# Writing a six-layer loop out, and moving one product and one normalisation in the drain of each layer

## The chip, the cores and the metric

The kernel runs on one core of a Trainium2 chip. The metric is device time in microseconds (us) of one execution. The core has five engines with an instruction stream each: TensorE (PE: matmuls, and PEld: its weight loads), VectorE (DVE), ScalarE (ACT), GpSimd (POOL) and SyncE (SP, which issues the DMAs). They meet through semaphores.

## The reference

Input x is 4 x 1024 tokens of width 128, all in float32. First comes one block of linear attention (16 heads, elu + 1 features) with a residual. Its layer-normalised result goes through a stack of six layers, and the stack's output is added to x:

```python
for i in range(6):
    x = attn_layer(shift_tokens(x), Wqkv[i], ...) + x      # 16 heads of 64, rotary, window of 32 plus the 32 before
    x = ffn_layer(shift_tokens(x), ln_g[i], ..., W2[i]) + x  # layer norm, 128 -> 2 x 341, a * gelu(gate), -> 128
```

In attn_layer q and k are l2-normalised, rotated, and the softmax runs over 64 keys for each query. shift_tokens delays half of the channels by one token.

## The kernel before

All x stays on the chip (x_tok). Work goes in tiles of 128 tokens: 32 tiles a layer (NT = 32), and for the feed-forward part in groups of four tiles (NG = 8).

**Front.** A software pipeline over the eight groups computes the linear attention. It holds small hardware loops of its own (schedule) and is not changed.

**Layers.** Every engine then runs its own hardware loop over the layers, `with engine.Fori(0, DEPTH) as l` (PE L476, DVE L920, ACT L1256, POOL L1519, SP L1663). The body is one layer, already written out tile by tile; only SP keeps inner loops. The layer number l is a register value, so semaphore targets such as NT * l + NT are computed in registers.

**Attention of a layer.** every_tile calls step(k) for k = 0 to 31 plus a drain of up to three more steps, and step(k) works on tile k in stage 0, tile k-1 in stage 1, and so on. Inside a step the order is written by hand on each engine; engines run in order and nothing reorders them. For tile 0 PE transposes the shifted tokens (L563), ACT and DVE split them into a high and a low part (xsT_hi, xsT_lo), PE projects q and k (L580 to L582), ACT squares them (L1324), DVE multiplies by the rotary tables (L1006, L1009) and makes the inverse norms, POOL adds and scales (L1542, L1551), PE transposes them (L594), computes scores (L632), and ACT takes exponentials (L1338), the first of them at k = 2. DVE and POOL normalise the probabilities (L993, L1531), PE transposes them (probs_transposed, L606), ACT copies them (p_evacuated), and PE multiplies by the values (output, L666). The values themselves come from products vo (L648), which ACT and DVE copy out of PSUM; a ring of four PSUM banks serves all these, so a product waits until its bank is copied.

**Drain and feed-forward.** Group 0 of the feed-forward part starts inside the drain. For group u: DVE centres it (L767, L769), ACT or DVE squares it, DVE takes the variance and a seed of the inverse root (L774 to L778), POOL runs twelve small Newton steps (group_rsqrt, L1454 to L1457), DVE writes the normalised tokens (normalised, L784), PE transposes them (L505), ACT and DVE split them, PE makes the up products up(u, par, i) for three blocks i of hidden columns (L525 to L527), ACT takes the gelu (L1396), DVE makes the hidden block (L1117), PE the down product (L539), and DVE the new x (L1125) with POOL's x plus bias xb (L1566).

In the drain PE runs up(0, 0, 0) at k = NT + 1, up(0, 0, 1) at k = NT + 2 ahead of the last tile's output, and up(0, 0, 2) after the residual of the last tile (x_mid). up(0, 0, 1) writes the two banks of the scores, so it waits for the last exponentials. DVE's normalised(0, 0) is called by every_tile ahead of step(NT + 1).

**Between layers.** The last products of a layer are wvo_product (L387), combined weights of the next layer; ACT copies them (wvo, L1161) and PE waits for all four copies before the next layer's first transpose.

**Activation tables.** ScalarE's functions sit in table sets. The build puts an ACT_TABLE_LOAD wherever the set that an instruction needs isn't known to be loaded there; at the head of a loop body nothing is known. Copy, Square and Identity run here under the set of Exp and under that of Gelu.

Of the kernel before, what the change touches and what calls it, by code (L numbers as in the profile page):

```python
# [35 lines left out]
NT = B * TPB  # L36
DEPTH, H, D, WIN = 6, 16, 64, 32
# [65 lines left out]
def build(nc, consts, at, x, Wq, bq, Wk, bk, Wv, bv, Wo, bo, Wqkv, q_scale, k_scale, Wout,  # L103
          ln_g, ln_b, W1, b1, W2, b2, out):
    ctx = ExitStack()
    with ctx:
# [217 lines left out]
        def every_tile(step, depth, before={}):  # L324

            for k in range(NT + depth):
                if k in before:
                    before[k]()
                step(k)
# [17 lines left out]
        def done(T):  # L347

            return passed(T + 1)
# [5 lines left out]
        def ahead(engine, value):  # L355

            engine.compute_val(value)
            return value
# [3 lines left out]
        def _(pe):  # L362
# [112 lines left out]

            with pe.Fori(0, DEPTH) as l:  # L476
                pe.wait_ge(x_ready, NT * l + NT)
# [67 lines left out]
                def step(k):  # L545
# [134 lines left out]
                    values(1, 1)  # L680
                    if k == NT + 2:
                        up(0, 0, 1)
                    output(3)
# [10 lines left out]
                    scores(0, 1)  # L694
                    probs_transposed(0, 2)
                    probs_transposed(1, 2)

# [36 lines left out]
        def _(dve):  # L734
# [184 lines left out]

            with dve.Fori(0, DEPTH) as l:  # L920
                dve.wait_ge(tables_ready, l + 1)
# [27 lines left out]
                def step(k):  # L949
# [149 lines left out]
                    rotate("k", 1, 0)  # L1099
                    softmax_bias(0, 1)  # L1100


# [40 lines left out]

                every_tile(step, 3, {NT + 1: lambda: normalised(0, 0)})

# [13 lines left out]
        def _(act):  # L1159
# [95 lines left out]

            with act.Fori(0, DEPTH) as l:  # L1256
                def step(k):
# [186 lines left out]
        def _(pool):  # L1444
# [46 lines left out]
            def tables(layer):  # L1491

                pool.wait_ge(sc_in, 32 * layer + 32)
                if not isinstance(layer, int):
                    pool.wait_ge(read["k"], done(NT * layer - 1))
                for n in range(4):
                    last = g.tensor_tensor(rotary[n][:, :].rearrange("p (j d) -> p j d", j=TPB), rotary0[:, n],
                                           qk_scales[:, n // 2, :].unsqueeze(1).broadcast_to([P, TPB, D]), ALU.mult)
                last.then_inc(tables_ready, 1)
# [18 lines left out]

            with pool.Fori(0, DEPTH) as l:  # L1519
                def step(k):  # L1520
# [82 lines left out]
        def _(sp):  # L1603
# [58 lines left out]
            for a in range(2):  # L1662
                attention_tokens(0, a, a, FT)  # L1663
            with sp.Fori(0, DEPTH) as l:

                layer = bass.ds(l, 1)
# [89 lines left out]
```

## Time and profile before

| | |
|---|---|
| median of 3 runs | 3485.94 us (3481.95 to 3488.68) |
| the profiled execution | 3480.63 us |
| its span in the trace | 3478.7 us |
| mean granted TensorE clock | 0.972 of full speed |
| instructions in the trace | 117627 |

The span runs from the first to the last instruction of the core. The profiled execution is one run of its own; it lies 5.31 us under the median of the three. Times of rows are counted from the start of the span. A layer takes some 554 us: about 450 us of steady tiles at 14 us, and the rest in the ramp at its head, the drain, the feed-forward part and the change to the next layer.

### The profile page before, as it was taken

The page shows a single profiled execution, that of the slowest core. Times are in us where ns is not written, and L with a number is a line of the kernel's source. Part 1 is how long each engine was busy: PE and PEld are TensorE (multiplying, and loading weights), DVE is VectorE, ACT ScalarE, POOL GpSimd, SP SyncE. Part 2 cuts the span into 40 slices and gives each one's busy share as a digit, 9 for nine tenths or more (in the row PEclk, how much of TensorE's full clock was granted, in tenths as well). Part 3 has the DMA queues.
Part 4 walks back from the last instruction along what each step waited for, and adds up shares of the span by engine and source line. Part 5 has one row for each costly group of instructions (what it writes and reads, how often), then busy time and mean ns, then how long its engine had stood idle before and what let it go on. Part 6 is the DMA issues. An engine that isn't in the chain of part 4 may idle for free.

```text
span 3478.7 us, 117627 instructions
## 1 busy us (share of the span) xinstructions
PE 3228.3 (93%) x42076; PEld 2192.2 (63%) x42076; DVE 2794.4 (80%) x5376; ACT 2933.6 (84%) x9251; POOL 2036.6 (59%) x2150
## 2 busy tenths in 40 slices
PE   5699999889999889999889999988999988999997
PEld 4466665756666656666566666575666666666666
DVE  7788888678888668888668888866888866888876
ACT  3399998579999659999849999867999975999984
POOL 3466666456666456665546666555666645666654
PEclk8799999999999999999999999999999999999999
DMA  2000000100000100000010000010000010000002
GB/s 72 10 7 7 13 7 5 45 15 7 13 7 6 44 15 7 13 8 7 11 46 7 7 13 7 5 45 15 7 13 7 7 40 18 7 9 11 7 8 64
DMA packets 141073, 57.78 MB, mean 17 GB/s; under 512 B 118598, under 2 KB 137668, under 8 KB 139460
## 3 DMA queue, kind: packets, MB, share of 16 engines
q1 hardware_dynamic: 140484, 50.01, 6.2%
q8 instruction: 360, 5.90, 0.7%
q14 instruction: 229, 1.88, 0.2%
HBM read 22.57 MB, written 2.10 MB: 7 GB/s over the span
## 4 chain that ended last, share of the span: by engine, by line
PE 70%; issue 9%; POOL 7%; DVE 7%; ACT 6%; POOLq 1%; DVEq 0%; DMA 0%; SPq 0%; ACTq 0%
PE ring L648 16%; PE ring L594 10%; PE ring L666 8%; PE s_ps L632 7%; PE qk_ps L580 6%; PE ring L606 5%; PE qk_ps L582 5%; PE qk_ps L581 5%; ACT probs L1338 3%; PE s_ps L636 2%; PE s_ps L623 2%; PE ring L539 1%; POOL ln_rs L1455 1%; POOL qk_rot L1551 1%; POOL xb L1566 1%
## 5 line engine op out<-in xcount | busy, mean ns | idle before, releaser
L1338 ACT ACTIVATE probs<-s_ps,nbias,rnorm 128x64 f32<-128x64 f32 x3072 | 1229.4, 446 | 1.6 <-DVE nbias L1059 0.2
L1542 POOL TENSOR_TENSOR qk_rot<-by_cos,by_sin 128x1024 f32<-128x1024 f32 x384 | 912.9, 2378 | 377.7 <-DVE by_sin L1009 325.4
L648 PE MATMUL ring<-wvo,xsT 128*32 128x512 f32 x6144 | 798.4, 602 | 10.2 <-ACT vo L1161 10.2
L1338 ACT ACTIVATION_READ_ACCUMULATOR probs<-s_ps,nbias,rnorm 128x1 f32 x3072 | 762.6, 248 | 0.0
L1531 POOL TENSOR_TENSOR probs<-probs,rrow 128x256 f32<-128x256 f32 x768 | 454.6, 613 | 337.4 <-DVE rrow L993 335.9
L1551 POOL TENSOR_TENSOR qk_rot<-qk_rot,rnorm 128x1024 f32<-128x1024 f32 x192 | 365.5, 1904 | 398.5 <-DVE rnorm L751 398.5
L1006 DVE TENSOR_TENSOR by_cos<-qk_ps,rotary 128x1024 f32<-128x1024 f32 x378 | 462.7, 1224 | 152.2 <-ACT squares L1324 152.2
L594 PEld LDWEIGHTS ring<-cst,qk_rot 128*128 128x128 f32 x3072 | 344.6, 142 | 290.5 <-ACT vo L1161 145.9
L594 PE MATMUL ring<-cst,qk_rot 128*128 128x128 f32 x3072 | 450.2, 280 | 74.1 <-POOL qk_rot L1542 49.7
L1021 DVE TENSOR_REDUCE sumsq<-squares 128x16 f32<-128x1024 f32 x384 | 462.5, 1204 | 0.0
L1009 DVE TENSOR_TENSOR by_sin<-qk_ps,rotary 128x1024 f32<-128x1024 f32 x378 | 458.5, 1213 | 0.0
L1324 ACT ACTIVATE squares<-qk_ps 128x1024 f32<-128x1024 f32 x378 | 398.3, 1054 | 40.0 <-PE qk_ps L582 40.0
L632 PE MATMUL s_ps<-kT,qT 128*32 128x128 f32 x10752 | 423.4, 279 | 0.0
L666 PEld LDWEIGHTS ring<-vo,pT 128*32 128x32 f32 x12288 | 345.1, 111 | 115.0 <-issue 114.6
L1161 ACT ACTIVATE kT<-ring 64x512 f32<-64x512 f32 x576 | 339.1, 589 | 41.7 <-PE ring L594 32.8
L666 PE MATMUL ring<-vo,pT 128*32 128x128 f32 x12288 | 373.4, 274 | 0.0
L580 PE MATMUL qk_ps<-wqk_hi,xsT_hi 128*128 128x512 f32 x756 | 341.6, 452 | 8.3 <-DVE xsT_lo L983 7.5
L1161 ACT ACTIVATE vo<-ring 128x512 f32<-128x512 f32 x576 | 326.4, 605 | 16.7 <-PE ring L648 2.5
L632 PEld LDWEIGHTS s_ps<-kT,qT 128*32 128x32 f32 x10752 | 284.9, 110 | 62.9 <-issue 62.2
L648 PEld LDWEIGHTS ring<-wvo,xsT 128*32 128x32 f32 x6144 | 157.8, 110 | 242.3 <-ACT vo L1161 156.3
L582 PE MATMUL qk_ps<-wqk_hi,xsT_lo 128*128 128x512 f32 x756 | 305.5, 404 | 0.0
L581 PE MATMUL qk_ps<-wqk_lo,xsT_hi 128*128 128x512 f32 x756 | 304.4, 403 | 0.0
(172 smaller groups left out, 5381.1 us busy)
## 6 DMA issues: line engine op xcount, KB each, us to landing
qk_rot<-L_ffn_Wqkv SPq DMA_DIRECT2D x7, 1024.0 KB, 5.1
xs<-x_tok SPq DMA_DIRECT2D x194, 32.0 KB
xs<-x_tok SPq DMA_DIRECT2D x194, 31.8 KB
wv<-L_ffn_Wqkv SPq DMA_DIRECT2D x7, 512.0 KB, 6.5
wo_pad<-L_ffn_Wo SPq DMA_DIRECT2D x14, 256.0 KB, 7.6
xs<-x_tok SPq DMA_DIRECT2D x194, 0.2 KB
xs_first<-x_tok SPq DMA_DIRECT2D x24, 128.0 KB
by_cos<-x_tok SPq DMA_DIRECT2D x24, 128.0 KB
```

Source lines behind the costliest of these rows:

```text
L580: mm(half, xsT_hi[:, a, :], wqk_hi[:, cols], start=True, stop=False)
L581: mm(half, xsT_hi[:, a, :], wqk_lo[:, cols], start=False, stop=False)
L582: last = mm(half, xsT_lo[:, a, :], wqk_hi[:, cols], start=False, stop=True)
L594: last = nc.tensor.transpose(r[:, p * P:(p + 1) * P], qk_rot[:, 1 if qk == "k" else 0, c:c + P], ident)
L632: last = mm(sc, q, keys[:, :, c:c + 2 * WIN], start=False, stop=True, skip_group_check=True)
L648: last = mm(r[WIN * mh:WIN * (mh + 1), :], xsT[:, a, WIN * w:WIN * (w + 1)], wvo[:, mh, :, :], start=True, stop=True)
L666: last = mm(r[WIN * w:WIN * (w + 1), 0:C], pT[:, quad, side, WIN * w:WIN * (w + 1)], vo[:, at_w, quad * C:(quad + 1) * C], start=(n == 0), ...
L1006: v.tensor_tensor(heads(by_cos[:, n, :]), heads(projection_banks(qk, k, s)), table.unsqueeze(1).broadcast_to([P, H, D]), ALU.mult)
L1021: v.tensor_reduce(sumsq[:, n * H:(n + 1) * H], heads(squares[:, n * INNER:(n + 1) * INNER]), AX, ALU.add).then_inc(summed[qk], 1)
L1161: return nc.scalar.activation(out_, in_, ACT.Copy)
L1338: last = nc.scalar.activation(probs[:, a, h // 4, :, h % 4, :], s_ps[:, half, c:c + 2 * WIN].rearrange("p (s c) -> p s c", s=2), ACT.Exp, ...
L1542: g.tensor_tensor(qk_rot[:, n, :], by_cos[:, n, :], by_sin[:, n, :], ALU.add).then_inc(added[qk], 1)
```

## The change

Three things. The five loops over the layers become Python loops, so that the six layers stand one behind the other in each engine's stream and l is a number. On PE up(0, 0, 1) moves from step NT + 2 (ahead of output) to step NT + 1, between the two probs_transposed. On DVE normalised(0, 0) is called as the last statement of step(NT) and no longer by every_tile ahead of step(NT + 1).

```diff
-                engine.compute_val(value)
+            if not isinstance(value, int):
+                engine.compute_val(value)
...
-            with pe.Fori(0, DEPTH) as l:          # and the same on DVE, ACT, POOL and SP
+            for l in range(DEPTH):
...
                     values(1, 1)
-                    if k == NT + 2:
-                        up(0, 0, 1)
                     output(3)
...
                     probs_transposed(0, 2)
+                    if k == NT + 1:
+                        up(0, 0, 1)
                     probs_transposed(1, 2)
...
                     softmax_bias(0, 1)
+                    if k == NT:
+                        normalised(0, 0)
...
-                every_tile(step, 3, {NT + 1: lambda: normalised(0, 0)})
+                every_tile(step, 3)
...
-                if not isinstance(layer, int):
+                if layer > 0:
                     pool.wait_ge(read["k"], done(NT * layer - 1))
```

## Rows read from the trace of the kernel before

**Rows 1.** The page's first part: busy us (share of the span) xinstructions.

```profile
PE 3228.3 (93%) x42076; PEld 2192.2 (63%) x42076; DVE 2794.4 (80%) x5376; ACT 2933.6 (84%) x9251; POOL 2036.6 (59%) x2150
```

**Rows 2.** Windows: one steady tile; length, busy by engine, PEclk, DMA share, GB/s.

```profile
914.87:928.90 14.03, 14.03 (x217) 9.25 (x217) 12.18 (x25) 13.78 (x48) 8.99 (x7) 1.00 0.13 28
```

**Rows 3.** Timeline of PE at loop boundaries: start, us, operation [idle before <-releaser].

```profile
700.96 0.34 PE L563 MATMUL ring<-cst,xs 128*128 128x128 f32 x1 [3.77 <-issue]
...
1254.23 0.47 PE L563 MATMUL ring<-cst,xs 128*128 128x128 f32 x1 [4.00 <-issue]
1255.87 0.77 PE L580 MATMUL qk_ps<-wqk_hi,xsT_hi 128*128 128x512 f32 x1 [1.17 <-DVE xsT_lo L983]
...
2917.69 0.47 PE L563 MATMUL ring<-cst,xs 128*128 128x128 f32 x1 [3.69 <-issue]
```

**Rows 4.** Timeline of ACT at the second boundary.

```profile
1250.27 0.60 ACT L1161 ACTIVATE wvo<-ring 128x512 f32<-128x512 f32 x1 [1.22 <-PE ring L387]
1253.83 1.28 ACT L1161 ACT_TABLE_LOAD   x1 [2.96 <-issue]
1255.12 0.28 ACT L1161 ACTIVATE xsT_hi<-ring 128x128 fp32r<-128x128 f32 x1
```

**Rows 5.** Groups by line: table loads; xcount, busy, mean ns, idle before by releaser.

```profile
L1161 ACT ACT_TABLE_LOAD x7 | 9.0, 1283 | 15.5 <-issue 14.7 <-PEq L1745 0.7
L1396 ACT ACT_TABLE_LOAD x6 | 7.7, 1283 | 0.1
```

**Rows 6.** Timeline of ACT at k = 2 of the third layer.

```profile
1278.64 0.60 ACT L1161 ACTIVATE qT<-ring 128x512 f32<-128x512 f32 x1 [0.90 <-PE ring L594]
1279.14 0.40 ACT L1338 ACTIVATE probs<-s_ps,nbias,rnorm 128x64 f32<-128x64 f32 x1
```

**Rows 7.** Timeline of PE at k = 2 of the third layer.

```profile
1285.50 1.06 PE L648 MATMUL ring<-wvo,xsT 128*32 128x512 f32 x8 [1.42 <-ACT vo L1161]
```

**Rows 8.** Timeline of ACT in the second layer's drain.

```profile
1175.06 0.28 ACT L1338 ACTIVATION_READ_ACCUMULATOR probs<-s_ps,nbias,rnorm 128x1 f32 x1
...
1178.23 0.60 ACT L1161 ACTIVATE pT<-ring 128x512 f32<-128x512 f32 x1 [1.08 <-PE ring L606]
1178.84 1.28 ACT L1396 ACT_TABLE_LOAD   x1
1180.14 0.69 ACT L1396 ACTIVATE by_sin<-qk_ps,b_col 128x512 f32<-128x512 f32 x1
```

**Rows 9.** Windows: the first projections of the third layer.

```profile
1255.80:1258.80 3.00, 2.93 (x7) 2.41 (x8) 0.00 (x0) 0.28 (x1) 0.00 (x0) 0.50 0.14 38
```

**Rows 10.** Timeline of PE in the second layer's drain.

```profile
1177.04 1.09 PE L606 MATMUL ring<-cst,probs 128*128 128x128 f32 x4 [2.55 <-POOL probs L1531]
1177.78 0.78 PE L525 MATMUL s_ps<-wqk_hi 128*128 128x512 f32 x1
...
1183.92 0.49 PE L525 MATMUL ring<-wqk_hi 128*128 128x512 f32 x1 [0.50 <-DVE x_tok L1068]
```

**Rows 11.** Timeline of DVE in the front, where semaphore targets are constants.

```profile
21.14 0.17 DVE L778 TENSOR_SCALAR ln_rs<-ln_rs 128x4 int32<-128x4 int32 x1
```

**Rows 12.** Timeline of POOL in the front.

```profile
21.39 0.20 POOL L1454 TENSOR_TENSOR ln_rs<-ln_rs 128x4 f32<-128x4 f32 x1 [4.44 <-DVE ln_rs L778]
```

**Rows 13.** Timeline of DVE, second layer's drain: seed of group 2, centre of group 3.

```profile
1180.95 0.17 DVE L778 TENSOR_SCALAR ln_rs<-ln_rs 128x4 int32<-128x4 int32 x1
...
1186.96 0.67 DVE L767 TENSOR_REDUCE ln_rs<-by_cos 128x4 f32<-128x512 f32 x1
```

**Rows 14.** Timeline of POOL in the same drain: first Newton step, then xb.

```profile
1181.20 0.20 POOL L1454 TENSOR_TENSOR ln_rs<-ln_rs 128x4 f32<-128x4 f32 x1 [4.30 <-DVE ln_rs L778]
...
1184.41 1.28 POOL L1566 TENSOR_TENSOR xb<-x_tok,b_row 128x512 f32<-128x512 f32 x1
```

**Rows 15.** Timeline of DVE in the third layer's drain: the same two operations.

```profile
1736.16 0.17 DVE L778 TENSOR_SCALAR ln_rs<-ln_rs 128x4 int32<-128x4 int32 x1
...
1741.38 0.67 DVE L767 TENSOR_REDUCE ln_rs<-by_cos 128x4 f32<-128x512 f32 x1
```

More of the change, by code:

```diff
@@ L917, in _ @@
             schedule(dve.Fori, step, 6, n=NG)
-            with dve.Fori(0, DEPTH) as l:
+            for l in range(DEPTH):
                 dve.wait_ge(tables_ready, l + 1)
@@ L1253, in _ @@
                 wvo_evacuated(r, 0)
-            with act.Fori(0, DEPTH) as l:
+            for l in range(DEPTH):
                 def step(k):
@@ L1516, in _ @@
             step(NG + 4, 0, None)
-            with pool.Fori(0, DEPTH) as l:
+            for l in range(DEPTH):
                 def step(k):
@@ L1663, in _ @@
                 attention_tokens(0, a, a, FT)
-            with sp.Fori(0, DEPTH) as l:
+            for l in range(DEPTH):
                 layer = bass.ds(l, 1)
```

## The prediction, on record before the changed kernel was run

> **What bounds the kernel now.** I read the page's busy shares first [rows 1]: PE is busy 93% and ACT 84%, too close for shares to decide, so the span has to be cut into stretches. In a steady tile PE is busy for the whole of its 14.03 us and ACT for 13.78 [rows 2]. Nothing of the change touches this stretch, so some 450 of a layer's 554 us stay as they are. That leaves three places: the change from one layer to the next, the ramp at the head of a layer, and the drain with the feed-forward part behind it. For these I read the timeline engine by engine.
>
> At a layer's end PE sits idle for 4.00 us before its first transpose with "issue" as the releaser, that is, waiting for nothing the profile shows; over the five boundaries this idle time is 3.77, 4.00, 3.57, 4.09 and 3.69 us, mean 3.82 [rows 3]. ACT shows the same hole, 2.96 us at this one, and then loads a table [rows 4]. Over the run that is 14.7 us of "issue" ahead of the seven loads of L1161 [rows 5]. Both engines lose the time just behind the end of their loop body.
>
> **The loops written out.** Three terms for each of five boundaries; the first layer has no layer ahead of it and gets none.
>
> *The hole.* ACT's last copy ends at 1250.27 + 0.60 = 1250.87 [rows 4], and PE must wait for that in any case. I allow 0.2 us for PE to react, an estimate. From PE's transpose to its first projection the trace has 1255.87 - 1254.23 = 1.64 us [rows 3]; the transpose is over at 1254.70, but the table load holds ACT until 1255.11, so 0.4 of it is the load, and 1.25 is left. The projection would start at 1250.87 + 0.2 + 1.25 = 1252.3 and not at 1255.87: 3.5 us sooner. The bounds are 0 (the hole has another cause and stays) and 4.5 (hole and load both vanish, with no reaction time). I take 3.5, near the upper end, since two engines show it at the same place and neither has anything to wait for. The other queues allow it: SP loaded the tokens of the first two tiles before its own loop closed, and POOL and DVE finish before ACT's last copy. What is late next is that copy.
>
> For the cause, which no row here names, there is the Trainium skill, "Runtime: NRT & Kernel Launch", section Instruction fetch mechanics: fetching runs ahead only along straight code, and a taken branch to a distant target waits for its page to be fetched.
>
> *The table load moves.* With l a number, the build knows at a layer's head that Gelu's set is loaded. Copy and Square run under it, so no load stands there; the first instruction that needs another set is the first Exp, at k = 2. There ACT has no slack: qT's copy is followed at once by the first exponential [rows 6], and a little later PE stands idle for 1.42 us until ACT has copied vo [rows 7]. A load of 1.28 us [rows 5] plus the lost overlap of 0.1 (the exponential starts 0.50 us after a copy of 0.60) makes 1.4 us, all of it on the path. Bounds: 0 (it fits into ACT's 0.90 us of idle time ahead of that copy) and 1.4; I take 1.4, as the load stands behind the copy. The first layer pays nothing: the front leaves Exp's set loaded.
>
> A rule speaks against this term. The trace's six loads ahead of a gelu start 0.01 us behind the copy and release the gelu 1.30 us later [rows 8]. The Trainium skill, "ScalarE: Activation LUTs", section What ACT_TABLE_LOAD costs, gives 2.66 us for a switch, a drain of 1.38 us included. By it the term would be 2.7 us and the whole gain 6.5 us smaller; by the rows it is 1.4. I go by the rows.
>
> *The clock.* The first projections run at a granted clock of 0.50 [rows 9], the lower level of 1.2 GHz, behind 4.00 and 1.17 us of idle time. Six of them, 0.43 us apart (seven in 3.0 us), lead to the first square; at twice the clock they take half, so up to 1.2 us could come back. With only 0.85 and 0.9 us of idle time ahead I give that a bit over one half: 0.7 us, bounds 0 and 1.2. Against it, PE's idle 1.42 us at k = 2 grows to 2.8, and in the drain 2.55 us of idle time was followed by slow products [rows 10]. I count 0.4 us for that, bounds 0 and 4.0 (the last rival, below, works out that end).
>
> A boundary gives 3.5 - 1.4 + 0.7 - 0.4 = 2.4 us, five of them 12 us.
>
> *Register arithmetic* goes too. In the front, where targets are constants, the first Newton step starts at 21.39, 0.08 us behind the end of the seed at 21.31 [rows 11, 12]. In a layer it is 1181.20 behind 1181.12: 0.08 again [rows 13, 14]. The arithmetic is done while the engine waits. I count 0; upper bound 2 us, lower bound 0, as nothing is added.
>
> **normalised(0, 0).** every_tile called it ahead of step(NT + 1); now it is the last statement of step(NT). Between the two stands nothing, so DVE's order of instructions is the same: 0 us, whatever its name says.
>
> **up(0, 0, 1) one step sooner.** PE is idle 2.55 us ahead of the last tile's second transposes at 1177.04 [rows 10]. The product needs the last exponentials, which end at 1175.34 [rows 8]. It could run from 1175.4, for 1.4 us at the high clock or 2.6 at the low one that is granted there, where the last transposes would begin 0.9 us late, at 1178.0. It is then no longer between the transposes and the output (before: 1177.78 to 1180.6), so output waits only for ACT's copy pT at 1178.23 to 1178.83 [rows 8], or 0.9 later. x_mid and up(0, 0, 2), at 1183.92 before [rows 10], come 0.9 to 1.8 us sooner. ACT's gelu load shifts with pT's copy and stays covered: the gelu that counts waits for up(0, 0, 2).
>
> But PE is not what the feed-forward part runs on. From the seed of group 2, fixed by ACT's last exponentials, POOL takes twelve Newton steps, then starts xb at 1184.41 [rows 14], and DVE cannot normalise group 2 before. DVE's write slows down while POOL runs xb. In the third layer, where the same drain got the high clock sooner, centring of group 3 starts 1741.38 - 1736.16 = 5.22 us behind the seed [rows 15]; in the second 1186.96 - 1180.95 = 6.01 [rows 13]. From the seed there are 3.46 us to xb and the slowed write, so 5.2 is a floor. Three of six layers (first, second, fourth) are like the second, three already at the floor: 3 x 0.8 = 2.4 us. Bounds: -1 (late transposes and a low clock in the fast layers) and 6 x 1.8 = 10.8. I take 2.
>
> **Sum.** 12 + 0 + 2 = 14 us. The profiled execution took 3480.63 us, its span 3478.7; it becomes 3466.6. The median of the three runs lies 5.31 us higher, so the forecast is 3472.
>
> **Rivals.**
> *The drain pays in full.* If the ring from seed to seed isn't the limit, x_mid's 1.6 us pass through in six layers: 9.6 for 2, and 3464. For it: PE idles on x_mid. Against it: the floor of 5.2 us [rows 13, 15].
> *The switch costs its drain too* (the rule above, as a mechanism): ACT is held for 2.7 us at k = 2. From the rows, 1.3 us more at five places: 3478. Against it: the gelu loads [rows 8].
> *The hole stays*, because it isn't the loop's. The load still leaves the head (0.4 back) and lands at k = 2 (1.4): 5 x 1.0 = 5 us worse, the drain 2 better: 3489. Against it: two engines, no releaser.
> *Slower: the moved load drops the clock.* At k = 2 PE is the bound from there on, and each us at half clock costs 0.5. The 2.8 us of idle time bring a low stretch of T us: from T / 2 = 3.5 - 1.4, so T = 4.2, a boundary loses, and with T = 8 and still slow first projections it is 5 x (3.5 - 1.4 - 4.0) = -9.5, with nothing from the drain: 3495. For it: the slow products behind 2.55 us [rows 10]. Against it: behind 1.42 us the clock stayed high here.
>
> **How the numbers follow.** Forecast 0.56 (its own range 3464 to 3481), drain in full 0.18, costly switch 0.10, hole stays 0.08, slower 0.08. The range of 3460 to 3484 leaves out the last two and a rest of some 0.04. A measurement of this kernel can tell about 0.2%, 7 us. Faster by more: 0.54 + 0.18 + 0.06 = 0.78; within: 0.02 + 0.04 + 0.08 = 0.14; slower 0.08.
>
> **What would show it.** Right: "issue" ahead of L563 falls from 3.8 us to under 1 us at five places; L1161 keeps one table load and L1338 gets five, each with about 1.3 us before the first exponential of layers two to six, PE's idle time ahead of L648 there near 2.8 us; s_ps products of L525 ahead of the last L606 in each drain; centring of group 3 at 5.2 us behind the seed in all six layers; the steady tile at 14.03. Wrong: an idle hole left at the boundary, a load still at the head, a steady tile of another length, or a centring closer than 5.0 us to the seed.

## The result and the profile after

The changed kernel takes 3454.74 us (median of 4 runs, 3454.36 to 3456.22); the kernel before, beside it, 3485.87 us (4 runs, 3481.95 to 3488.68). The ratio is 0.9912, 95% interval 0.9900 to 0.9925: 31 us faster, where 14 were forecast (3472, range 3460 to 3484). The sign was right, the time lies outside the range on the fast side.

The profiled execution took 3454.96 us, its span is 3453.06 us against 3478.73, so 25.7 us of span are gone. The page's first line, against [rows 1], shows where not to look: PE lost 23 us of busy time and is at 93% as before.

```profile
PE 3204.9 (93%) x42076; PEld 2183.8 (63%) x42076; DVE 2797.3 (81%) x5376; ACT 2928.4 (85%) x9250; POOL 2035.8 (59%) x2150
```

I cut both spans at the same instructions of every layer and summed over the six layers (negative is sooner). These differences of start times are the ledger for all that follows:

| part of the layer, from / to | forecast | measured |
|---|---|---|
| boundary: last wvo copy's end / first token transpose (five) | -15.5 (5 x 3.5, less 0.4 each behind the transpose) | -15.4 |
| ramp: that transpose / first output product | +3.5 (5 x (1.4 + 0.4 - 0.7 - 0.4)) | +7.6 |
| steady tiles: first output product / last token transpose | 0 | **-16.3** |
| last tiles: that transpose / last exponential | 0 | -3.4 |
| drain and feed-forward part: last exponential / last wvo copy | -2 | +1.3 |
| ahead of the first layer, behind the last | 0 | +0.5 |
| sum | -14 | -25.7 |

**The boundary.** The timeline of PE and that of ACT at the second boundary (start, us, operation, idle before and its releaser), against [rows 3, 4]:

```profile
1247.20 0.30 PE L564 MATMUL ring<-cst,xs 128*128 128x128 f32 x1 [0.73 <-issue]
1248.35 0.47 PE L581 MATMUL qk_ps<-wqk_hi,xsT_hi 128*128 128x512 f32 x1 [0.85 <-DVE xsT_lo L984]
...
1249.12 0.40 PE L581 MATMUL qk_ps<-wqk_hi,xsT_hi 128*128 128x512 f32 x1
```

```profile
1246.50 0.60 ACT L1164 ACTIVATE wvo<-ring 128x512 f32<-128x512 f32 x1 [1.22 <-PE ring L388]
1247.53 0.28 ACT L1164 ACTIVATE xsT_hi<-ring 128x128 fp32r<-128x128 f32 x1 [0.43 <-PE ring L564]
```

4.00 us of "issue" became 0.73, and the transpose starts 0.10 us behind ACT's last copy at all five boundaries. The trace also records each engine's queue (its branches, waits and register operations), which the views above leave out. There the hole starts at the branch that closes the loop: in the kernel before ACT's branch at 1250.34 us ends at 1250.39, and the next record of its queue is at 1253.75. At the five boundaries this gap is 2.95 to 3.58 us on ACT, 2.72 to 2.85 on DVE and 2.50 to 2.64 on POOL; DVE and POOL have it earlier and are through it before ACT's last copy ends. The changed kernel has no such gap on these engines. The two L581 rows are 0.77 us apart for three products, against 0.43 us for one in [rows 9]: here the first projections run at the high clock. In one other layer they do too, in three they don't.

**k = 2.** The groups of table loads by line, against [rows 5], and the timelines of ACT and PE at k = 2 of the third layer, against [rows 6, 7]:

```profile
L1399 ACT ACT_TABLE_LOAD x6 | 7.7, 1283 | 0.1
L1341 ACT ACT_TABLE_LOAD x5 | 6.4, 1283 | 0.1
L1164 ACT ACT_TABLE_LOAD x1 | 1.3, 1283 | 0.7 <-PEq L1748 0.7
```

```profile
1269.32 0.60 ACT L1164 ACTIVATE qT<-ring 128x512 f32<-128x512 f32 x1 [0.80 <-PE ring L595]
1269.94 1.28 ACT L1341 ACT_TABLE_LOAD   x1
1271.23 0.40 ACT L1341 ACTIVATE probs<-s_ps,nbias,rnorm 128x64 f32<-128x64 f32 x1
```

```profile
1277.61 1.31 PE L649 MATMUL ring<-wvo,xsT 128*32 128x512 f32 x8 [2.85 <-ACT vo L1164]
1278.86 1.12 PE L595 MATMUL ring<-cst,qk_rot 128*128 128x128 f32 x4
```

The load moved as forecast, and the five loads hold ACT for 1.3 us each. PE's idle time grew from 1.42 to 2.85 us (forecast 2.8), but behind it the clock falls: the first row below is the stretch after it, the second the first projections of the same layer (windows: length, busy by engine, then PEclk, DMA share, GB/s).

```profile
1278.80:1281.40 2.60, 2.60 (x12) 2.24 (x9) 1.53 (x3) 1.98 (x7) 1.18 (x2) 0.50 0.00 0
...
1248.30:1249.80 1.50, 1.45 (x6) 1.24 (x7) 0.00 (x0) 0.27 (x1) 0.00 (x0) 1.00 0.15 7
```

I call a time at the granted clock of 0.50 (1.2 GHz) a low stretch. This one comes in all five layers and costs 1.4 to 1.6 us each time, not 0.4 (worked out from e7_exp_early, below, where it is gone).

**The steady tile.** Six tiles of the second layer by windows, before and after (before is a new row):

```profile
835.75:919.86 84.11, 84.11 (x1236) 55.04 (x1235) 73.28 (x146) 82.68 (x277) 53.97 (x43) 1.00 0.06 12
```

```profile
833.64:917.20 83.56, 83.56 (x1237) 55.02 (x1235) 72.71 (x146) 82.48 (x277) 53.92 (x42) 1.00 0.06 12
```

PE is "busy" for every last hundredth of both, with the same products at the same clock, and yet one is 0.55 us shorter. So PE did wait in the first, and the busy column hid it: ends of matmuls are modelled, and a pause of 0.1 us vanishes under the end of the row before. It shows in start times only. POOL and PE around one tile's start, before:

```profile
874.14 1.18 POOL L1531 TENSOR_TENSOR probs<-probs,rrow 128x256 f32<-128x256 f32 x2 [1.77 <-DVE rrow L993]
875.49 2.38 POOL L1542 TENSOR_TENSOR qk_rot<-by_cos,by_sin 128x1024 f32<-128x1024 f32 x1 [0.16 <-PE ring L594]
...
877.79 0.27 PE L563 MATMUL ring<-cst,xs 128*128 128x128 f32 x1
878.01 0.63 PE L594 MATMUL ring<-cst,qk_rot 128*128 128x128 f32 x4
```

and after:

```profile
871.76 1.19 POOL L1534 TENSOR_TENSOR probs<-probs,rrow 128x256 f32<-128x256 f32 x2 [1.64 <-DVE rrow L994]
873.01 2.37 POOL L1545 TENSOR_TENSOR qk_rot<-by_cos,by_sin 128x1024 f32<-128x1024 f32 x1
...
875.40 0.27 PE L564 MATMUL ring<-cst,xs 128*128 128x128 f32 x1
875.53 0.63 PE L595 MATMUL ring<-cst,qk_rot 128*128 128x128 f32 x4
```

From POOL's last normalised probabilities to its add of q it is 1.35 us before and 1.25 after; from PE's token transpose to its first q transpose, which waits for that add, 0.22 and 0.13. In the kernel before the add waits against three register values, and POOL's queue records show what that does. One tile earlier the last probabilities end at 861.29 us; the queue's first wait starts at 861.27, a register operation of 0.03 us at 861.33, the add at 861.46. In the changed kernel the queue's wait starts at 857.78, while the probabilities (to 859.00) are still running, and the add starts at 859.07. So with constants the waits are read ahead. That the length of the tile hangs on this pause is a theory until experiments bear it out.

**The drain.** DVE in the second layer, seed of group 2 and centre of group 3, against [rows 13]:

```profile
1177.44 0.17 DVE L779 TENSOR_SCALAR ln_rs<-ln_rs 128x4 int32<-128x4 int32 x1
...
1182.71 0.67 DVE L768 TENSOR_REDUCE ln_rs<-by_cos 128x4 f32<-128x512 f32 x1
```

5.27 us for 6.01: the centring is at the floor of 5.2 in five of six layers (5.6 in the fifth). The up product starts 0.14 us behind the last exponential, output 1 to 2 us sooner than before. But from one group's centring to the next (the period) it is now 8.70 us for 8.64, four times a layer, and from the last centring to the last wvo copy 28.9 us for 28.6.

**The last tiles.** Their 3.4 us are the clock's: in three layers of the kernel before it is low there for twice as long (41.7 to 42.1 us) as in the other three (40.6 to 40.8); in the changed kernel all six are like the latter (40.7 to 41.0).

### The profile page after: what moved, and what is told of

Same layout as the page of the kernel before. It is cut to its first block, busy times and chain, and to the rows that moved or that the text cites. A ratio compares the mean times of both kernels' runs of the same rounds, so it can differ in the third digit from the quotient of the medians.

```text
span 3453.1 us, 114079 instructions
## 1 busy us (share of the span) xinstructions
PE 3204.9 (93%) x42076; PEld 2183.8 (63%) x42076; DVE 2797.3 (81%) x5376; ACT 2928.4 (85%) x9250; POOL 2035.8 (59%) x2150
## 4 chain that ended last, share of the span: by engine, by line
PE 66%; DVE 11%; ACT 11%; POOL 6%; issue 5%; DVEq 0%; DMA 0%; SPq 0%; ACTq 0%; POOLq 0%
PE ring L649 16%; PE ring L595 9%; PE ring L667 7%; PE s_ps L633 7%; ACT probs L1341 6%; PE qk_ps L581 5%; PE ring L607 4%; PE qk_ps L582 4%; PE qk_ps L583 4%; PE s_ps L637 2%; DVE xn L785 2%; PE s_ps L624 2%; PE ring L540 1%; POOL qk_rot L1554 1%; POOL ln_rs L1458 1%
## 5 line engine op out<-in xcount | busy, mean ns | idle before, releaser
L649 PE MATMUL ring<-wvo,xsT 128*32 128x512 f32 x6144 | 801.7, 605 | 18.1 <-ACT vo L1164 17.9
L1341 ACT ACTIVATION_READ_ACCUMULATOR probs<-s_ps,nbias,rnorm 128x1 f32 x3072 | 771.3, 251 | 0.0
L581 PE MATMUL qk_ps<-wqk_hi,xsT_hi 128*128 128x512 f32 x756 | 342.8, 453 | 5.2 <-DVE xsT_lo L984 5.1
L649 PEld LDWEIGHTS ring<-wvo,xsT 128*32 128x32 f32 x6144 | 158.1, 110 | 249.3 <-ACT vo L1164 163.7
```

The costliest lines, as they stand in the source:

```text
L581: mm(half, xsT_hi[:, a, :], wqk_hi[:, cols], start=True, stop=False)
L649: last = mm(r[WIN * mh:WIN * (mh + 1), :], xsT[:, a, WIN * w:WIN * (w + 1)], wvo[:, mh, :, :], start=True, stop=True)
L1341: last = nc.scalar.activation(probs[:, a, h // 4, :, h % 4, :], s_ps[:, half, c:c + 2 * WIN].rearrange("p (s c) -> p s c", s=2), ACT.Exp, ...
```

## The experiments

All times are medians; each ratio is against runs of the kernel before on the same chip, whose medians were 3485.5 to 3487.6 us.

### Which part of the change gives what

**e1_loops_only**: the loops alone.

```
-                    if k == NT + 1:
-                        up(0, 0, 1)
                     probs_transposed(1, 2)
...
+                    if k == NT + 2:
+                        up(0, 0, 1)
                     output(3)
```

> The changed kernel with up(0, 0, 1) put back where it was (called in step(NT + 2) ahead of output(3)); the loops stay written out. Theory A, the drain rests on the ring from seed to seed of the feed-forward groups and the earlier product gives almost nothing: within 2 us of the changed kernel's 3454.7, that is 3453 to 3457. Rival B, the drain pays in full (1.6 us in six layers): 3464. Centring of group 3 at 11.6 us behind the last exponential in three layers, as in the kernel before, by A; x_mid late by 1.6 us but nothing behind it.

3457.93 us (ratio 0.9919, 0.9906 to 0.9932). The loops alone bring 29.6 us by their own pair of medians, against 31 for the whole change; directly compared, the two medians are 3.2 us apart. That is much nearer to A, a little above its range, than to B. In its trace the centring comes 11.75 to 11.85 us behind the last exponential in five layers, and 10.88 in the changed kernel: the moved product gives 0.9 us there, and loses part of it again, because here the first projections of four layers run at the high clock and in the changed kernel those of two.

**e2_up_only**: the kernel before with the product moved.

```
-                    if k == NT + 2:
-                        up(0, 0, 1)
                     output(3)
...
+                    if k == NT + 1:
+                        up(0, 0, 1)
                     probs_transposed(1, 2)
```

> The kernel before with only the up product moved; every loop is still a loop. Theory A: 0 to 2.4 us faster, 3483.5 to 3486. Rival B (x_mid's 1.6 us pass through in six layers): 3476. By A the steady tile and the idle time ahead of L564 stay as before (3.8 us at five boundaries).

3476.10 us (ratio 0.9969, 0.9957 to 0.9980): 11 us, where I had 0 to 2.4 and the rival 10. The trace doesn't support the rival's mechanism: the centring is at 10.84 to 10.86 us in all six layers, the floor, and what x_mid gains (0.5 to 2.4 us a layer against the first profile) does not pass through. That B named the time is luck. The drain gives 1.6 us. To see the rest a second execution of the kernel before was profiled.

**b2_before_again**: the kernel before, nothing changed.

> The kernel before once more, unchanged, for a second profiled execution: the first one took 3480.6 us, 5 to 7 us less than the median. Theory K: an execution nearer to the median differs in low clock stretches of PE alone, 1.5 us at a time, in the last tiles and in the drain, where output and up(0, 0, 1) run late and centring of group 3 at 11.6 us in more than three layers; steady tiles without such a stretch take the same 84.11 us for six. Rival L: the whole execution is slower evenly.

3485.81 us, span 3483.9. Against the first profile (3478.7) six tiles take the same 84.1 us; the difference is in stretches at low clock: one more of 1.5 us in the steady tiles, 1.2 us more in one layer's last tiles, the rest in the ramps and ahead of the first layer. Theory K holds for the place, but centring is late in two layers only, where K had more than three. Against this execution e2's profiled span, 3475.1, is 8.8 us shorter: drain 1.6, last tiles 2.7, ramps 2.6, steady tiles 1.6. So some 7 of these 8.8 us lie outside the drain, in parts where e2 has fewer or shorter low stretches of PE's clock. Why the moved product brings them no run tells.

**e3_pool_only**: the kernel before, one engine's loop written out.

```
-            with pool.Fori(0, DEPTH) as l:
+            for l in range(DEPTH):
```

> The kernel before with only GpSimd's layer loop written out. Theory C, the steady tile is a ring through all engines and one link of it is the pause of POOL between the last normalised probabilities and the add of q, which shrinks with constant wait targets (0.16 to 0.07 us, seen in the two traces): some 30 tiles of six layers at 0.09 us, 16 us faster, 3470; tiles 10 to 16 of a layer take 83.6 us and not 84.1; the boundary's hole of 3.8 us stays. Rival D, it is PE's own register-valued waits or another engine's: 3486, nothing gained.

3474.26 us (ratio 0.9969, 0.9958 to 0.9980): 11 to 13 us, where C had 16. D is out. POOL's start to start is 1.26 us, the 3.8 us holes stay, and six tiles take 83.59 us. Tiles 4 to 10 fall by 0.22 us only, where the changed kernel has 0.82, and a layer's steady tiles give 1.5 us (layers without a low stretch) of the changed kernel's 2.5.

**e4_all_but_pool**: the changed kernel with POOL's loop put back.

```
-            for l in range(DEPTH):
+            with pool.Fori(0, DEPTH) as l:
```

> The changed kernel with GpSimd's layer loop kept as a loop, all others written out, the up product moved. Theory C: the steady tiles are as slow as before, 16 us more than the changed kernel, 3471; the boundary's hole is gone all the same. Rival D: 3455. If POOL's own back edge is late at a boundary it shows as a wait of DVE or PE on POOL behind it; none is expected, POOL has no work there for some microseconds.

3474.75 us (ratio 0.9963, 0.9950 to 0.9976), 20 us above the changed kernel. Tiles 10 to 16 take 84.10 us again and POOL's pause is 0.16. The boundary is at 0.10. By the ledger 9.5 of the 20 us are in the steady tiles; 7.0 are in the last tiles (41.9 us a layer for 40.7), where the clock is now low for twice as long in every layer. The other engines' loops together bring 0.6 us a layer of the steady tiles' 2.5 (low stretches of the clock taken out: the kernel before has two there, the changed one has one, this one none); where, I haven't traced.

**e5_pe_act_only** and **e6_pe_only**: the kernel before with the loops of PE and ACT, or of PE alone, written out.

> The kernel before with only PE's and ACT's layer loops written out; POOL, DVE and SP keep theirs, the up product stays. Theory O: the hole at the boundary is the back edges of these two; it is gone (3.1 us a boundary), Exp's load moves to k = 2 with its low clock (2.8 us back), the steady tile stays at 84.1 us for six: 5 x 0.3 plus what the first projections gain from the clock, some 3 to 9 us: 3478 to 3485, taken 3480. Rival P: the hole needs all five loops gone (DVE's or SP's edge is late next): 3.1 us a boundary stay and the load still moves, 3495.

> The kernel before with PE's layer loop alone written out. Theory O: PE transposes the first tokens 3 us sooner, and then waits for ACT, whose own back edge still stands: 0.2 to 1 us a boundary, 3483 to 3487. Rival Q: PE's edge alone makes the hole and ACT's hides behind it: 5 x 3 us less, with no load moved, 3472.

With both: 3477.37 us (10 runs, ratio 0.9977, 0.9968 to 0.9986); every boundary at 0.10 us, the load at k = 2, in four of the five layers with a low stretch behind it, six tiles at 84.11. O holds, its time just above the measured one, and P is out. PE alone: 3482.21 us (11 runs, ratio 0.9992, 0.9983 to 1.0001), nothing that can be told from no change; Q is out. Its profiled execution, at 3473.18 us, is the fastest of the eleven, so only the boundary is read from it. PE's own hole is gone and it waits for ACT's instead, as PE and ACT show at its second boundary:

```profile
1251.44 0.30 PE L564 MATMUL ring<-cst,xs 128*128 128x128 f32 x1 [0.73 <-issue]
1256.27 0.76 PE L581 MATMUL qk_ps<-wqk_hi,xsT_hi 128*128 128x512 f32 x1 [4.53 <-DVE xsT_lo L984]
```

```profile
1254.23 1.28 ACT L1162 ACT_TABLE_LOAD   x1 [2.89 <-issue]
1255.53 0.28 ACT L1162 ACTIVATE xsT_hi<-ring 128x128 fp32r<-128x128 f32 x1
```

Each of the two engines pays some 3 us for its own back edge (the branch back to the head of the loop), both at the same time, and taking away PE's alone gives next to nothing: what the boundaries gain (15.4 us in all) the ramps lose again but for 2.9.

### The steady tile

**e9_split_add**: the kernel before, loops kept, the add in two halves.

```
+                        if qk == "q":
+                            for half in range(2):
+                                h = slice(512 * half, 512 * half + 512)
+                                pool.wait_ge(qT_ps[half], done(T - 1))
+                                if half == 0:
+                                    pool.wait_ge(read["q"], done(T))
+                                g.tensor_tensor(qk_rot[:, 0, h], by_cos[:, 0, h], by_sin[:, 0, h], ALU.add
+                                                ).then_inc(added["q"] if half else added_first, 1)
+                            return
...
-                        pe.wait_ge(k_rotated if qk == "k" else added["q"], done(T))
+                        pe.wait_ge(k_rotated if qk == "k" else added["q"] if half else added_first, done(T))
```

> The kernel before, all loops kept as loops, with POOL's add of q in two halves of 128x512, each with a semaphore of its own, so that PE's first q transposes wait for the first half alone (1.2 us sooner). Theory C (the steady tile of the kernel before is the ring POOL's add of q, PE's transposes; relieving it in any way frees it, until PE itself is the bound): six tiles fall from 84.1 to 83.5 us, about 16 us in all, 3471; PE's pause between L563 and L594 falls from 0.17 to 0.11 us. Rival J, what the written out loop of POOL gave was something else than this link (its other waits, its fetches): 3486 or more, since the split adds an instruction of POOL per tile.

3460.40 us (ratio 0.9931, 0.9917 to 0.9946): 27 us, with every loop still a loop, where C had 16. By the ledger, against the first profile, 12.4 us are in the steady tiles and 11.1 in the last tiles, which C had left out. PE and six tiles:

```profile
876.00 0.27 PE L564 MATMUL ring<-cst,xs 128*128 128x128 f32 x1
876.11 0.60 PE L595 MATMUL ring<-cst,qk_rot 128*128 128x128 f32 x4
```

```profile
834.34:917.70 83.36, 83.36 (x1237) 55.13 (x1236) 73.01 (x146) 82.27 (x277) 54.54 (x48) 1.00 0.06 12
```

PE's start to start is 0.11 us and six tiles take 83.36 us, less than in the changed kernel: the link is POOL's add. Where it is gone PE looks like the bound (0.11 us is the least that the pair shows in any run). In layers with one low stretch the last tiles fall from 40.8 to 39.7 us.

**e10_after_split**: the same edit on the changed kernel.

> The changed kernel with POOL's add of q in two halves (the same edit as in the split on the kernel before). Theory M: the changed kernel's steady tile is the same ring, only with a shorter pause; six tiles fall from 83.57 to 83.36 us, where PE is the bound, the last tiles by 1.1 us a layer as they did there; about 2 us a layer, 12 in all: 3443. Rival N: with constant targets PE is already the bound and the split gives nothing: 3455.

3439.38 us (ratio 0.9870, 0.9853 to 0.9887), 15 us below the changed kernel. Six tiles take 83.35 us, which is what M says, but five layers now have a low stretch further on, worth 1.2 to 1.5 us, which takes the gain of the steady tiles back. The 15 us are in the last tiles (2.7 us less in five layers, 38.0 each; the clock does not fall there, and in the sixth, where it does, the gain is 0.8) and in the ramps (3.8 in all). M holds as to the link; its sum of 12 came out by other terms.

**e13_extra_wait**, **e14_tiny_op** and **e15_real_pause** try to lengthen the pause in the changed kernel and read the tile.

```
+                            pool.wait_ge(added["q"], done(T - 1))
+                            pool.wait_ge(added["k"], done(T - 1))
+                            pool.wait_ge(k_rotated, done(T - 1))
+                            pool.wait_ge(kT_ps[0], done(T - 2))
```

> The changed kernel with four more waits of POOL ahead of its add of q in each tile, all on counts that were reached long before (POOL's own adds of the tile before, and older transposes), so that nothing is waited for and only the pause between the last normalised probabilities and the add grows, by one or two separate wait instructions. Theory S, the pause itself sets the tile's length: the tile grows by as much as POOL's pause does (each 0.06 us more would be some 11 us in all: 3466, or 3477 for two). Rival T, the pause is covered and POOL's written out loop works by something else: 3455.

3455.59 us (ratio 0.9914), the same. But POOL's start to start is 1.26 us, as without them: four waits that are long satisfied cost nothing (in POOL's queue they are read 1.1 us and more ahead of the add), so no dose was given and S is not tested.

```
+                            pool.wait_ge(tiny, done(T - 1))
+                            g.memset(bq_minus[:, :], 0.0).then_inc(tiny, 1)
```

> The changed kernel with a memset of 128x1 on POOL between the last normalised probabilities and the add of q in each tile (0.1 us by the memsets of that size in POOL's start-up), so that the pause really grows; the four satisfied waits of the run before left it at 0.07 us and measured nothing. Theory S: the add starts about 0.1 us later behind the probabilities and each tile of the steady state grows by nearly that: six tiles 84.1 to 84.3 us for 83.57, some 17 to 22 us in all, 3472 to 3477. Rival T, the pause is covered: 83.57 and 3455.

3452.51 us (ratio 0.9906). The memset starts beside the end of the probabilities' operation and moves the add by 0.01 us. Again no dose.

```
+                            pool.wait_ge(tiny, done(T - 1))
+                            pool.wait_ge(p_normed[1], done(T))
+                            g.tensor_tensor(bq_minus[:, :], bq_minus[:, :], bq_minus[:, :], ALU.subtract).then_inc(tiny, 1)
```

> The changed kernel with one small POOL operation (128x1 minus itself) ahead of the add of q in each tile, and this operation waits for the end of the last normalised probabilities, so that it can't slip in beside them as the memset did (that moved the add by 0.01 us only, and the tile by 0.006). By Newton's steps, which wait for one another, it costs 0.2 to 0.28 us. Theory S: the pause grows from 0.07 to 0.3 us and more, and each steady tile by as much less what PE had in hand (0 to 0.05): six tiles 84.8 to 85.3 us for 83.57, 37 to 55 us in all, 3492 to 3510. Rival T, the pause is covered by PE's work: 83.57 and 3455.

3493.68 us (11 runs, ratio 1.0022, 1.0013 to 1.0031), 39 us above the changed kernel. POOL, then PE, then six tiles:

```profile
881.62 1.18 POOL L1535 TENSOR_TENSOR probs<-probs,rrow 128x256 f32<-128x256 f32 x2 [1.80 <-DVE rrow L995]
882.95 0.19 POOL L1540 TENSOR_TENSOR bq_minus<-bq_minus 128x1 f32<-128x1 f32 x1
883.10 2.37 POOL L1550 TENSOR_TENSOR qk_rot<-by_cos,by_sin 128x1024 f32<-128x1024 f32 x1
...
885.27 0.27 PE L565 MATMUL ring<-cst,xs 128*128 128x128 f32 x1
885.61 0.63 PE L596 MATMUL ring<-cst,qk_rot 128*128 128x128 f32 x4
```

```profile
842.58:927.73 85.15, 84.52 (x1236) 55.04 (x1235) 73.07 (x146) 83.33 (x277) 54.88 (x49) 1.00 0.06 12
```

Start to start on POOL grew by 0.23 us (1.25 to 1.48), PE's wait from 0.13 to 0.34, and the tile by (85.15 - 83.56) / 6 = 0.27 us here, 0.22 in layers at 84.9. S holds: of each 0.1 us of POOL's pause the tile pays 0.1. Only now does the busy column fall below the length (84.52 of 85.15); the likely reason is that the pause has outgrown the modelled ends.

### The table load, and the feed-forward groups

**e7_exp_early**: the changed kernel with a tiny Exp where ACT is idle.

```
                     wvo_evacuated(r, l + 1)
+                    if r == 1:
+                        nc.scalar.activation(bq_minus[:, :], bq_col[:, :], ACT.Exp)
```

> The changed kernel with one tiny Exp (128x1, into a buffer not used any more) on ACT behind the second wvo copy of each layer's end, where ACT is idle for 1.2 to 1.6 us between copies, so that Exp's table set is loaded there and not at k = 2 on the path. Theory E: the load at k = 2 (about 1.3 us) and most of the low clock that follows PE's 2.85 us of idle time there (1.5 us) go in five layers: 14 us, 3441. Rival F: the low clock stays, since PE's idle time only shrinks to 1.5 us and something else brings it: 5 x 1.3 = 6.5 us, 3448. Rival G: the load delays the next copy and the layer's end by as much: 3450 to 3455.

3443.39 us (3440.44 to 3451.60, ratio 0.9888, 0.9871 to 0.9906): 11 us below the changed kernel by the medians. The five runs fall into two sets, three at 3440 to 3443 and two at 3451 to 3452 with a lower mean clock, so the size is known to a few us only; the profiled execution is of the first set. ACT at the layer's end, and PE at k = 2:

```profile
1242.90 0.60 ACT L1164 ACTIVATE wvo<-ring 128x512 f32<-128x512 f32 x1 [0.97 <-PE ring L388]
1243.52 1.28 ACT L1445 ACT_TABLE_LOAD   x1
1244.81 0.20 ACT L1445 ACTIVATE bq_minus<-bq_col 128x1 f32<-128x1 f32 x1
1245.10 0.60 ACT L1164 ACTIVATE wvo<-ring 128x512 f32<-128x512 f32 x1
```

```profile
1277.94 1.06 PE L649 MATMUL ring<-wvo,xsT 128*32 128x512 f32 x8 [1.49 <-ACT vo L1164]
```

The load is hidden, PE's idle time is back at 1.49 us, and L649 takes 1.06 us, the high clock. Between the two copies around the load it is 2.20 us with and without it, so G is out. The ramp, which was 43.2 to 44.5 us, is 40.3 to 41.6: E, not F. Like with like (first projections at the high clock, 43.2 and 40.3; at the low one, 44.5 and 41.6) the moved load costs 2.9 us a layer, a little over half of it through the clock. The five ramps give 15.6 us by the ledger; one more low stretch in the steady tiles takes 2.5 of them back.

**e8_wait_order** and **e11_square_order** ask why the groups went from 8.64 to 8.70 us.

```
-                    dve.wait_ge(g_xnT_ps, done(U - 1))
                     counted = U + 1 if u == 0 else U
-                    scaled(...)
+                    dve.wait_ge(norm_g["rsqrt"], passed(NEWTON_OPS * (counted + 1)))
+                    dve.wait_ge(g_xnT_ps, done(U - 1))
+                    scaled(..., True)
```

> The changed kernel with the two waits ahead of the normalised groups' write (L785) in the other order, Newton's steps first, so that the instruction itself carries the wait that is released last and the one on PE's transposes stands in a separate instruction ahead. Theory H: the write starts 0.07 us sooner behind POOL's last step, the group's period in the feed-forward part falls from 8.70 to 8.64 us as in the kernel before, 0.4 us a layer, 2.5 us in all: 3452. Rival I, the longer period has another cause (registers of another engine): 3454.7, period 8.70.

3454.86 us, nothing, and the period is 8.72. The write does start sooner behind Newton's last step, by 0.07 us, but it takes 1.73 us for 1.66: it runs beside POOL's xb, and in both kernels it ends 1.81 us behind xb's start. H fell.

The timelines then showed the lost 0.06 us on ACT: from the start of the centring's second operation (DVE) to the Square's, 0.72 us before and 0.79 after.

```profile
1196.32 0.69 DVE L769 SCALAR_TENSOR_TENSOR by_cos<-ln_rs,by_cos 128x512 f32<-128x512 f32 x1
...
1197.04 0.63 ACT L1377 ACTIVATE squares<-by_cos 128x512 f32<-128x512 f32 x1 [2.73 <-DVE by_cos L769]
```

```profile
1192.12 0.69 DVE L770 SCALAR_TENSOR_TENSOR by_cos<-ln_rs,by_cos 128x512 f32<-128x512 f32 x1
...
1192.91 0.63 ACT L1380 ACTIVATE squares<-by_cos 128x512 f32<-128x512 f32 x1 [3.71 <-DVE by_cos L770]
```

```
-                    act.wait_ge(norm_g["var"], done(U - 1))
                     act.wait_ge(norm_g["centred"], done(U))
+                    act.wait_ge(norm_g["var"], done(U - 1))
                     nc.scalar.activation(squares4, ...
```

> The changed kernel with ACT's Square of the feed-forward groups waiting on the centring first and on the variance second, and nothing else. Theory R: the group's period falls from 8.70 to 8.64 us, the part from the last exponential to the last wvo copy from 75.28 to 75.0 us as it did beside the other two edits, 1.8 us in all: 3453. Rival U: it came from the other edits there: 3454.7 and 75.28.

3455.68 us (3451.89 to 3457.17), which can't be told from the changed kernel's time, but the trace shows the step: centring to Square 0.72 us again (1189.57 and 1190.29), the period 8.65, and the part from the last exponential's end to the last copy 75.1 us in all six layers, where the changed kernel has 75.28 in four, 75.31 and, in the fifth, 75.64. R holds in the trace, some 1.1 us in all for 1.8, too small for the timing. The 0.3 us that the layer's end lost behind the last centring stay (28.86 us); 0.13 of them come with PE's loop alone (28.75 in e6), and no run tells more.

**e12_all_three**: early Exp, split add, order of the Square's waits.

> The changed kernel with the tiny Exp at the layer's end (11 us less, measured), the split add of q (12 us by theory M) and, in ACT's Square of the feed-forward groups, the wait on the centring ahead of the one on the variance, so that the Square itself carries the wait released last. Theory R for the latter: with constant targets the instruction carries the first wait and a separate instruction of 0.06 us the second; the Square starts 0.06 us sooner behind the centring, the group's period falls from 8.70 to 8.64 us, 2 us in all. Sum: 3430. If N holds: 3441; if the period stays at 8.70: 3432.

3421.16 us (3420.07 to 3426.99, ratio 0.9820, 0.9807 to 0.9834): 64 us below the kernel before and 34 below the changed one, the fastest of all. The single gains (11, 15 and, by the trace, 1) add to 27; six tiles are at 83.4 us, the period at 8.64, the ramp at 40.3 to 41.5. Against e10's trace the ramps are 11.2 us shorter, the drains 2.1 and the steady tiles 3.8, where two layers have a low stretch and not five; the last tiles are 2.8 longer, since the clock falls there in two layers and not in one. By the traces that is 15 us, by the medians 18, for a sum of 12: most of what exceeds it lies in where the clock falls, and why it falls less often in the steady tiles no run tells.

## Why the prediction was wrong

**The failed step: "Nothing of the change touches this stretch, so some 450 of a layer's 554 us stay as they are."** It took PE's busy time of 14.03 in 14.03 us [rows 2] for proof that PE bounds the tile. The tile was a ring through POOL's add, with a pause of 0.1 us in it that the written out loop takes away (e3, e4), that a split add takes away without it (e9), and that lengthens the tile one for one when it grows (e15). Over the six layers the steady tiles gave 16.3 us, 1.5 of them one low stretch less, the rest the tile's own (some 0.6 us a layer of it by the loops of other engines, untraced, e4); that is more than the whole forecast. Without them the profiled execution's 25.7 us would be 9.4, less than the 14 forecast. The prediction had named "a steady tile of another length" as a sign of being wrong, and it is: 13.93 us for 14.02.

**The step from the profile to the median.** The sum was taken from the profiled execution and then raised by 5.31 us, the amount by which the kernel before lay above its own profile. The changed kernel's median lies 0.22 us below its profiled execution. So 5.5 of the 17.2 us between forecast and measurement are this step, and 11.7 the terms (25.7 for 14). The kernel before varies from run to run by its low stretches (b2); the changed one varies by under 2 us in its four runs, and nothing in the sum allowed for that.

**The last tiles** were put at nothing too, and gave 3.4 us, by the clock.

**Register arithmetic.** "The arithmetic is done while the engine waits", 0 us, upper bound 2. The rows for it [rows 11 to 14] were two places where the engine does wait, for something that comes last. At the add POOL waits for nothing: its queue gets there when the probabilities are done, and then every step of it is on the path. The bound was drawn from rows of the harmless kind. That the register targets make the pause, and nothing else of POOL's loop, is read from the queue records; no run keeps the loop with constant targets.

**The hole.** Right: 3.1 us a boundary, five times, the last copy late next, two engines paying at once (e5, e6). *The hole stays* is out. The Trainium skill, "Runtime: NRT & Kernel Launch", section Instruction fetch mechanics, has a taken branch to a distant target wait for the fetch of its page. The runs agree in that the hole starts at the branch and goes engine by engine with the loop, 2.5 to 3.6 us without a record in the queue; that a fetch fills it no run here shows.

**The table load.** Right in place and size: 1.3 us for 1.4, 0.02 us behind the copy, and the exponential 0.01 us behind the load. *The switch costs its drain too* is out; the Trainium skill, "ScalarE: Activation LUTs", section What ACT_TABLE_LOAD costs, has 2.66 us, and all 12 loads of this trace take 1.28, with no further pause around the five at k = 2.

**The clock.** Mis-sized, and here the slower rival was half right: I counted 0.4 us for the longer idle time at k = 2, it is 1.4 to 1.6 in five layers (e7 gives it back). The first projections got 1.2 us in two layers of five, where I had 0.7 in each of the five. A boundary with its ramp gave 1.6 us and not 2.4: 8 for 12.

**normalised(0, 0)**: DVE's order is the same, 0 us, as said.

**up(0, 0, 1).** The floor was right (10.88 us in five of six layers), and so was the part of the term that rests on it: 1.6 us on the kernel before by the trace, for 2. But the runs give 11 us there and 3 on the written out loops; by the traces most of what goes beyond the drain lies in stretches at low clock, which my sum had left out. *The drain pays in full* has a time near that by another way, x_mid's gain doesn't pass through. In the changed kernel the drain ended 1.3 us longer than before, since a layer lost 0.55 us there whatever the product did: 0.06 us in each of four periods (e11 gives most of that back) and 0.3 behind the last centring (open). That is 3.3 us, and the product gave 2.0.

**The range.** It was built from the prices of the edits that I saw. Nothing in it stood for a part of the kernel that I had declared untouched, though constant targets touch every wait of every engine.

## What to carry to other kernels

A busy share of 100% is no proof of a bound where ends are modelled: compare the starts of the same two instructions over several tiles, and ask for each wait on the ring which engine's pause it stands behind. When all loops are written out, every wait with a register target changes; here the one mattered whose engine arrives just in time, not those where it has long been waiting. A forecast built on one profiled execution should say how far that execution lies from the median, and should not carry that distance over to the changed kernel. And where an edit moves a load or a wait to a place at which PE already idles, price the clock that falls behind it, at full.

## What the runs showed of the hardware

- A back edge costs its engine some 3 us: 2.96 us of "issue" on ACT in [rows 4] and 2.89 beside PE's straight code in e6. PE's hole goes with its own loop alone. In the queues the gap behind the branch is 2.5 to 3.6 us on ACT, DVE and POOL.
- Waits on constants that are satisfied are read ahead while the engine works (four more: 0.00 us, e13); waits on register values behind the same operation cost 0.09 us (a pause of 0.16 us for 0.07, e4 and e3). A memset of 0.10 us slipped in beside the operation before it (0.01 us, e14). An operation that waits for that one's end cost 0.23 us (e15).
- Of two waits ahead of one instruction, the order in the program costs 0.06 to 0.07 us when the one that is released last stands second (0.79 for 0.72 us on ACT, e11; 0.15 for 0.08 on DVE, e8).
- DVE's write ends at a time set by POOL's xb beside it, 1.81 us behind its start, whether it began 0.08 or 0.15 us behind it (e8).
- The kernel before spreads over 3476.6 to 3491.8 us in all its runs, the changed one over 3454.4 to 3456.2 in its four; two profiles of the kernel before differ by low clock stretches of 1.2 to 1.5 us.
